# The place of a two-column sum in TensorE's queue: after the first transpose of a group, or in front of the product of its third tile

## The chip, the cores and the metric

One Trainium2 chip, one of its cores. The metric is the device time of the kernel in microseconds (us); less is better. Engines are called by their short names: PE (TensorE), DVE (VectorE), ACT (ScalarE), POOL (GpSimd) and SP (SyncE, which issues the loads). Line numbers (L1210) are those of the kernel before.

## The reference

The input `x` has 16 channels of 2048 x 2048 float32, in 8 groups of two channels. Two layers follow one another:

```python
# layer 0: group norm, causal mask, depthwise 6 x 11 convolution, mask, residual
xm = jnp.where(causal_mask, gn(x), 0)
y  = conv(xm, weight, padding=((5, 0), (5, 5)), feature_group_count=C)
x  = x + jnp.where(causal_mask, y, 0)
# layer 1: group norm again, plus a bias that depends on (row - column) only
m, s = mean(x_group), var(x_group)
x  = x + (x - m) / sqrt(s + 1e-5) + table[row - column]
```

Each of the two normalisations needs a mean and a variance over a whole group (two channels). The "second statistics" are those of layer 1: they can be had only when the last tile of the group has been through the convolution.

## The kernel before

A channel is cut into 4 bands of 512 rows, each band into overlapping tiles of 128 columns; only tiles that touch the lower triangle are convolved. That makes NT = 90 tiles for a group and 720 in all, numbered N = 90 g + n. The engines work as a pipeline in a common order written out by hand: `stage(s)` runs over n = 0 to 89, and in it a group s is being loaded and measured (its first statistics), group s-1 is being convolved, and group s-2 is finished (second normalisation, bias, store). So each stage has one seam, where the tiles of one group end and those of the next begin.

For each tile: ACT normalises it into `xn` (L647, four tiles ahead), POOL multiplies the mask into it where the tile lies on the diagonal (L1084), PE transposes it into `psT` (L1170, two tiles ahead), ACT copies the result as float16 into `XT` (`split_hi`, L659), DVE writes the rest of the float32 value beside it (`split_lo`, L801), POOL copies the halo columns (L1099, L1110), PE multiplies (the "product", 36 matmuls, L1184, into one of three `psY`), and DVE masks and adds the result to x (`evict`, L814 and L816). DVE also takes the first statistics from loaded buffers (L829) and does part of the finishing (L991, L1002). ACT squares and sums the finished blocks (`piece`, L679).

PE's queue takes tiles in triples. For a triple that begins at tile N it is: transpose N+2, product N, transpose N+3, product N+1, transpose N+4, product N+2. The product of tile N waits for `split_lo` of tile N and for the eviction of tile N-3; the transpose of tile N waits for its `xn` and for `split_lo` of tile N-3.

What ties the seam together, with "first" for the first tile of the new group:

- DVE, at n = 0: evict the old group's last tile, `split_lo` of tile first+2, sum of the tiles' sums (L924), one pair of L829. At n = 1 (STATS2): `stats2` part 0 (L935 to L944; waits for ACT's last squares, ends with the increment of `s2_chain` that PE waits for), then `split_lo` of tile first+3 (L801), then `stats2` part 1 (L949 on, waits for `s2_summed`), part 2 (the inverse root, with ACT's square root L753 in the middle, then L959, L960 and the shift of the kept bias, L964), then the eviction of tile first.
- ACT, at n = 1: the last squares (`piece`), `split_hi` of tile first+3, the norm of tile first+5, the square root, the shift of the bias (L699). At n = 2: `split_hi` of tile first+4.
- PE: `sum_results` (L1210) multiplies the two columns of `t2` by a matrix of ones, which sums them over the 128 partitions. In the trace it is two matmul records.
- SP: the loads go in order into a ring of 8 buffers of 512 KB (L566), beside the kept blocks (L572) and the bias (L602); a load waits for its buffer's last use.

There are 8 sums of this kind. Seven of them (groups 0 to 6) are issued in the first triple of the following group; the last stands alone at the end of PE's queue.

Of the kernel before, what the change touches and what calls it, by code (L numbers as in the profile page):

```python
# [25 lines left out]
def preact_conv_kernel(nc, x, wflip, w1, b1, w2, b2, w3, b3, out):  # L26
# [23 lines left out]
    NB3 = 3  # L50
# [257 lines left out]
    with ctx:  # L308
# [839 lines left out]
        def _(pe):  # L1148
# [16 lines left out]
            def transpose(N, m):  # L1165

                wait(pe, lo_ready, N - NB3 + 1)
                pe.wait_ge(xn_ready, N + 1)
                for i in range(NPC):
                    last = nc.tensor.transpose(psT[m][:, i, :], xn[:, m, i, :, :].rearrange("p k c -> p (k c)"), ident[:, :])  # L1170
                last.then_inc(transposed, 1)

            def convolve(N, m, c):
                pe.wait_ge(lo_ready, N + 1)
                pe.wait_ge(halo_in, N + 1)
                wait(pe, evicted, N - NB3 + 1)
                products = [(i, sh, xp, wp) for i in range(NPC) for sh in range(3)
                            for xp, wp in ((0, 0), (0, 1), (1, 0))]
                for j, (i, sh, xp, wp) in enumerate(products):
                    lo_c = max(0, PADC - XC * i)  # L1180
                    hi_c = min(WC, TOUT + PADC - XC * i)
                    rows = min(K, NE - K * sh)
                    o = XC * i - PADC
                    last = nc.tensor.matmul(psY[m][:, 0:rows, o + lo_c:o + hi_c],  # L1184
                                            XT[:, m, xp, i, 2 - sh:2 - sh + P],
                                            wsplit[:, c, wp, K * sh:K * sh + rows, lo_c:hi_c],
                                            start=(j == 0), stop=(j == len(products) - 1), skip_group_check=True)
                last.then_inc(convolved, 1)

            def triple(N, c, ahead=NB3, results_of=None):  # L1190

                for i in range(NB3):
                    if i < ahead:
                        transpose(N + i + 2, (i + 2) % NB3)
                    if i == 0 and results_of is not None:
                        sum_results(results_of)
                    convolve(N + i, i, c)

# [9 lines left out]
            def sum_results(g):  # L1208
                pe.wait_ge(s2_chain, 13 * g + 4)
                nc.tensor.matmul(total[:, 2:4], ones[:, :], t2[:, 0:2], start=True, stop=True).then_inc(s2_summed, 1)  # L1210

            def group(g, before, after):

                first = NT * g
                pe.wait_ge(w_built, chan(g, 0) + 1)
                triple(first, 0, results_of=g - 1 if before else None)
                with pe.Fori(1, NTC // NB3) as j:
                    triple(first + NB3 * j, 0)
                pe.wait_ge(w_built, chan(g, 1) + 1)
                triple(first + NTC, 1)  # L1220
                with pe.Fori(NTC // NB3 + 1, SUM1[0] if after else 2 * NTC // NB3 - 1) as j:
                    triple(first + NB3 * j, 1)
                if after:
                    triple(first + NB3 * SUM1[0], 1)
                    sum_means(g + 1)
                    triple(first + NB3 * SUM1[1], 1)
                    sum_variances(g + 1)
                    with pe.Fori(SUM1[1] + 1, 2 * NTC // NB3 - 1) as j:
                        triple(first + NB3 * j, 1)
# [37 lines left out]
```

## Time and profile before

| | |
|---|---|
| time, median of 3 runs | 2635.06 us (2629.83 to 2635.5) |
| the profiled execution: its own time | 2638.45 us |
| its span, first to last instruction | 2636.7 us |
| DVE busy | 2304.3 us, 87% |
| PE busy | 1979.8 us, 75% |
| ACT busy | 1660.3 us, 63% |
| POOL busy | 1260.7 us, 48% |
| moved by DMA | 894.88 MB, mean 339 GB/s |
| mean granted clock of PE | 0.912 of full speed |

How to read it: the shares are means over the span. A stage of the middle lasts 313 us or so, and which engine holds it changes inside the stage, so the table alone says nothing of a seam. Rows of the timeline give the start and the length of an instruction (or of several alike, with their count), and in brackets the idle time of its engine before it and what ended it.

### The profile page before, as it was taken

The numbers are of one execution on the slowest core, as the hardware profiler recorded it, in microseconds if no ns is written. First come the engines' busy times: TensorE is split into PE (matmuls) and PEld (weight loads), VectorE is DVE, ScalarE is ACT, GpSimd is POOL, SyncE is SP. The second block draws the span as 40 slices with busy tenths as digits, with TensorE's granted clock in tenths as the row PEclk, the third lists the DMA queues.
The fourth block names the chain that finished last, engine by engine and source line by source line (L and its number), as shares of the span: only waits on it lengthen the run. The fifth ranks groups of instructions, "written<-read, shape, count | busy, mean of one in ns | idle before, by whom it ended". The sixth has DMA issues, their size and how long they took to land. (4 is left out here: it accounts for less than half of the span.)

```text
span 2636.7 us, 76763 instructions
## 1 busy us (share of the span) xinstructions
PE 1979.8 (75%) x28880; PEld 1876.5 (71%) x28880; DVE 2304.3 (87%) x4175; ACT 1660.3 (63%) x3051; POOL 1260.7 (48%) x1988
## 2 busy tenths in 40 slices
PE   4289988888687876878778877888868778899800
PEld 0289887878687776877778776787768778899800
DVE  7799988899888997899888998889988899778846
ACT  2167766766576675766667666666656757687722
POOL 1123235535545454454555445554554546475543
PEclk9999998999899999999898999999889998999955
DMA  9775649999899998999989998999989997797999
GB/s 337 273 243 170 233 136 384 393 371 351 329 408 377 380 337 332 402 359 385 354 334 396 359 366 329 378 392 362 348 329 395 384 373 297 284 355 274 334 370 360
DMA packets 313546, 894.88 MB, mean 339 GB/s; under 512 B 42272, under 2 KB 42272, under 8 KB 311296
## 3 DMA queue, kind: packets, MB, share of 16 engines
q1 hardware_dynamic: 198528, 576.64, 59.3%
q10 hardware_dynamic: 114832, 316.22, 31.0%
q8 instruction: 60, 0.98, 0.1%
q14 instruction: 126, 1.03, 0.1%
HBM read 576.36 MB, written 316.53 MB: 339 GB/s over the span
## 5 line engine op out<-in xcount | busy, mean ns | idle before, releaser
L1184 PEld LDWEIGHTS psY<-wsplit,XT 128*128 128x128 f16 x25920 | 1607.2, 102 | 355.9 <-DVE XT L801 128.6
L1184 PE MATMUL psY<-wsplit,XT 128*128 128x168 f16 (+5 forms) x25920 | 1635.9, 223 | 290.7 <-DVE XT L801 240.2
L659 ACT CAST XT<-psT 128x512 f16<-128x512 f32 x720 | 414.8, 576 | 561.0 <-PE psT L1170 325.5
L1110 POOL COPY halo<-XT 128x16 f16<-128x16 f16 x720 | 318.9, 443 | 657.5 <-DVE XT L801 647.3
L801 DVE TENSOR_TENSOR XT<-psT,XT 128x512 f16<-128x512 f32 x720 | 493.8, 686 | 140.3 <-ACT XT L659 139.4
L1084 POOL TENSOR_TENSOR xn<-xn,mask 128x512 f32<-128x512 f32 x336 | 423.7, 1261 | 387.5 <-ACT xn L647 325.8
L829 DVE BATCH_NORM_STATS2 entries<-ring 128x6 f32<-128x512 f32 x872 | 551.4, 679 | 61.3 <-DMA ring<-in_x 61.0
L1170 PE MATMUL psT<-ident,xn 128*128 128x128 f32 x2880 | 480.3, 292 | 98.2 <-POOL xn L1084 77.6
L1119 POOL TENSOR_TENSOR ring<-ring,bias 128x1024 f32<-128x1024 f32 x181 | 408.4, 2258 | 253.7 <-ACT ring L708 253.6
L647 ACT ACTIVATE xn<-kept_c_band,normp 128x512 f32<-128x512 f32 (+2 forms) x496 | 398.4, 803 | 48.3 <-DMA kept_c_band<-in_x 26.9
L1170 PEld LDWEIGHTS psT<-ident,xn 128*128 128x128 f32 x2880 | 317.8, 146 | 107.4 <-POOL xn L1084 72.5
L816 DVE SCALAR_TENSOR_TENSOR kept_c_band<-psY,wback,kept_c_band 128x472 f32<-128x472 f32 (+3 forms) x496 | 342.5, 691 | 14.2 <-PE psY L1184 7.3
L679 ACT ACTIVATE junk<-kept_c_band,cur 128x512 f32<-128x512 f32 (+2 forms) x464 | 311.6, 672 | 49.5 <-DVE kept_c_band L816 26.2
L991 DVE SCALAR_TENSOR_TENSOR kept_c_band<-kept_c_band,outp,bias 128x1024 f32<-128x1024 f32 x224 | 329.2, 1478 | 11.6 <-ACT bias L699 11.6
L708 ACT ACTIVATE ring<-ring,outp 128x1024 f32<-128x1024 f32 x181 | 206.0, 1140 | 124.1 <-DMA ring<-in_x 48.0
L814 DVE TENSOR_TENSOR psY<-psY,mask 128x472 f32<-128x472 f32 (+2 forms) x336 | 202.8, 604 | 11.7 <-PE psY L1184 11.4
L1002 DVE SCALAR_TENSOR_TENSOR ring<-ring,outp,bias 128x1024 f32<-128x1024 f32 x101 | 173.9, 1724 | 33.2 <-DMA ring<-in_x 24.3
L1099 POOL COPY XT<-halo 128x16 f16<-128x16 f16 x720 | 159.9, 222 | 51.4 <-PE psY L1184 47.4
L647 ACT ACTIVATE xn<-band,normp 128x512 f32<-128x512 f32 (+1 forms) x224 | 174.3, 779 | 13.9 <-DVE normp L911 13.9
L816 DVE SCALAR_TENSOR_TENSOR band<-psY,wback,band 128x472 f32<-128x472 f32 (+2 forms) x224 | 150.4, 671 | 6.3 <-PE psY L1184 0.7
L679 ACT ACTIVATE junk<-band,cur 128x512 f32<-128x512 f32 x192 | 131.9, 687 | 36.3 <-DVE band L816 27.1
L679 ACT ACTIVATION_READ_ACCUMULATOR junk<-kept_c_band,cur 128x1 f32 x464 | 87.1, 188 | 0.0
(81 smaller groups left out, 486.2 us busy)
## 6 DMA issues: line engine op xcount, KB each, us to landing
ring<-in_x SPq DMA_DIRECT2D x628, 512.0 KB, 8.6
out<-ring ACTq DMA_DIRECT2D x282, 512.0 KB, 6.1
kept_c_band<-in_x SPq DMA_DIRECT2D x224, 512.0 KB, 8.1
out<-kept_c_band ACTq DMA_DIRECT2D x224, 512.0 KB, 7.0
band<-in_x SPq DMA_DIRECT2D x48, 1024.0 KB, 11.3
out<-band ACTq DMA_DIRECT2D x45, 1024.0 KB, 8.7
ring<-out SPq DMA_DIRECT2D x90, 512.0 KB, 9.5
bias<-bias_scratch SPq DMA_DIRECT2D x16, 1793.5 KB, 8.5
```

The costliest lines, as they stand in the source:

```text
L647: last = nc.scalar.activation(to[:, :, 0:whole, :], slot(c, b)[:, :, x0:x0 + XC * whole].rearrange("p k (i c) -> p k i c", c=XC), ACT.Iden ...
L659: nc.scalar.copy(XT[:, n % NB3, 0, :, 2:P + 2], psT[n % NB3][:, :, :]).then_inc(hi_ready, 1)
L679: nc.scalar.activation(junk[:, 0:nr * (c1 - c0)].rearrange("p (r c) -> p r c", r=nr), slot(c, b)[:, r:r + nr, BW * q + c0:BW * q + c1], AC ...
L801: nc.vector.tensor_tensor(XT[:, n % NB3, 1, :, 2:P + 2], psT[n % NB3][:, :, :], XT[:, n % NB3, 0, :, 2:P + 2], ALU.subtract).then_inc(lo_r ...
L816: nc.vector.scalar_tensor_tensor(out=xs, in0=y, scalar=col(wback, c), in1=xs, op0=ALU.mult, op1=ALU.add, accum_out=sums[:, n:n + 1]).then_ ...
L829: last = nc.vector.bn_stats(entries[:, e, :], row(q, r))
L991: nc.vector.scalar_tensor_tensor(out=v, in0=v, scalar=col(outp, 0), in1=bias_at(blk, nr // 2 * h, nr // 2), op0=ALU.mult, op1=ALU.add).the ...
L1084: nc.gpsimd.tensor_tensor(v, v, m, ALU.mult).then_inc(xn_ready, 1)
L1110: nc.gpsimd.tensor_copy(halo[:, t, :, :, :], XT[:, n % NB3, :, :, P:P + 2]).then_inc(halo_out, 1)
L1119: nc.gpsimd.tensor_tensor(v, v, bias_at(STREAM[u]), ALU.add).then_inc(u_added, 1)
L1170: last = nc.tensor.transpose(psT[m][:, i, :], xn[:, m, i, :, :].rearrange("p k c -> p (k c)"), ident[:, :])
L1184: last = nc.tensor.matmul(psY[m][:, 0:rows, o + lo_c:o + hi_c], XT[:, m, xp, i, 2 - sh:2 - sh + P], wsplit[:, c, wp, K * sh:K * sh + rows, ...
```

## The change

In `triple`, the sum is issued in front of the third product instead of the first. PE's queue in the first triple of groups 1 to 7 was: transpose first+2, sum, product first, transpose first+3, product first+1, transpose first+4, product first+2. It becomes: transpose first+2, product first, transpose first+3, product first+1, transpose first+4, sum, product first+2. Nothing else is changed: no other engine's queue, no wait, no buffer.

```diff
@@ -1192,7 +1192,7 @@
                 for i in range(NB3):
                     if i < ahead:
                         transpose(N + i + 2, (i + 2) % NB3)
-                    if i == 0 and results_of is not None:
+                    if i == NB3 - 1 and results_of is not None:
                         sum_results(results_of)
                     convolve(N + i, i, c)
```

## Rows read from the trace of the kernel before

**Rows 1.** Windows: the stage between the sums at 998 and 1311 us.

```profile
core 0: us, PE busy (x) PEld busy (x) DVE busy (x) ACT busy (x) POOL busy (x), PEclk, DMA share, GB/s
997.80:1311.30 313.50, 247.41 (x3606) 235.69 (x3606) 284.06 (x521) 205.45 (x379) 160.18 (x247) 0.92 0.96 364
```

**Rows 2.** Timeline of PE across the seam at 685 us.

```profile
674.23 0.64 PE L1170 MATMUL psT<-ident,xn 128*128 128x128 f32 x4
...
676.67 0.64 PE L1170 MATMUL psT<-ident,xn 128*128 128x128 f32 x4
685.03 0.58 PE L1210 MATMUL total<-t,ones 128*128 128x2 f32 x2 [7.72 <-DVE t L944]
685.48 3.76 PE L1184 MATMUL psY<-wsplit,XT 128*128 128x148 f16 x36
689.07 1.10 PE L1170 MATMUL psT<-ident,xn 128*128 128x128 f32 x4
...
696.82 2.13 PE L1184 MATMUL psY<-wsplit,XT 128*128 128x148 f16 x36 [1.69 <-DVE band L816]
```

**Rows 3.** Timeline of DVE, ACT and POOL across the same seam.

```profile
676.69 0.69 DVE L801 TENSOR_TENSOR XT<-psT,XT 128x512 f16<-128x512 f32 x1
...
679.79 0.69 DVE L801 TENSOR_TENSOR XT<-psT,XT 128x512 f16<-128x512 f32 x1
...
681.07 1.12 POOL L1084 TENSOR_TENSOR xn<-xn,mask 128x512 f32<-128x512 f32 x1 [2.95 <-ACT xn L650]
...
683.08 0.52 ACT L679 ACTIVATE junk<-kept_c_band,cur 128x310 f32<-128x310 f32 x1
...
684.83 0.15 DVE L944 SCALAR_TENSOR_TENSOR t<-t 128x1 f32<-128x1 f32 x1
...
690.82 0.69 DVE L801 TENSOR_TENSOR XT<-psT,XT 128x512 f16<-128x512 f32 x1 [5.85 <-ACT XT L659]
691.43 0.15 DVE L949 TENSOR_SCALAR t<-total 128x1 f32<-128x1 f32 x1
...
693.72 0.16 DVE L960 SCALAR_TENSOR_TENSOR outp<-t 128x1 f32<-128x1 f32 x1
```

**Rows 4.** Timelines of DVE at the six other seams, the same instruction.

```profile
379.07 0.69 DVE L801 TENSOR_TENSOR XT<-psT,XT 128x512 f16<-128x512 f32 x1 [5.85 <-ACT XT L659]
...
1003.59 0.69 DVE L801 TENSOR_TENSOR XT<-psT,XT 128x512 f16<-128x512 f32 x1 [5.85 <-ACT XT L659]
...
1316.42 0.69 DVE L801 TENSOR_TENSOR XT<-psT,XT 128x512 f16<-128x512 f32 x1 [5.16 <-ACT XT L659]
...
1630.10 0.69 DVE L801 TENSOR_TENSOR XT<-psT,XT 128x512 f16<-128x512 f32 x1 [5.42 <-ACT XT L659]
...
1944.49 0.69 DVE L801 TENSOR_TENSOR XT<-psT,XT 128x512 f16<-128x512 f32 x1 [5.13 <-ACT XT L659]
...
2253.41 0.69 DVE L801 TENSOR_TENSOR XT<-psT,XT 128x512 f16<-128x512 f32 x1 [5.86 <-ACT XT L659]
```

**Rows 5.** Windows after the seams at 998 and 2248 us, columns as in rows 1.

```profile
1007.80:1012.80 5.00, 3.32 (x51) 2.85 (x49) 4.93 (x13) 3.88 (x6) 0.02 (x1) 1.00 0.15 35
...
1002.80:1032.80 30.00, 23.11 (x349) 21.43 (x348) 28.27 (x57) 18.10 (x29) 16.67 (x19) 0.98 0.73 243
...
1037.80:1057.80 20.00, 14.11 (x215) 13.73 (x212) 13.04 (x24) 11.71 (x23) 7.59 (x14) 0.86 1.03 416
...
2247.60:2262.60 15.00, 13.62 (x175) 13.31 (x176) 8.36 (x24) 6.49 (x9) 1.79 (x5) 0.80 0.10 39
```

**Rows 6.** Waits over the span (us, times, longest), then timelines of DVE and PE.

```profile
DVE entries L829 <- DMA ring<-in_x: 61.0, 41, 6.1
...
1052.74 1.29 DVE L829 BATCH_NORM_STATS2 entries<-ring 128x6 f32<-128x512 f32 x2 [6.08 <-DMA ring<-in_x]
...
1055.72 3.54 PE L1184 MATMUL psY<-wsplit,XT 128*128 128x148 f16 x36 [3.87 <-DVE XT L801]
```

**Rows 7.** L602 alone, the bias load issued at 677.80 us.

```profile
DMA to landing us min/median/max: 10.0/10.0/10.0
```

## The prediction

> **What bounds the kernel now.** I read the page first, for the busy shares, then windows of whole stages. In a middle stage DVE works 284.06 of 313.5 us and the DMA engines are busy 0.96 of the time, while PE works 247.41 [rows 1]. So two things share the bound, DVE and the transfers. Windows of 5 to 30 us show that they take turns. In the 30 us behind the seam at 998 us DVE is busy 28.27 us and the DMA share is 0.73; from 1037.8 us the share is 1.03, which is as full as this trace gets over 20 us, and DVE falls to 13.04 of 20 us, waiting among other things 6.08 us for a load of the ring [rows 5, 6]. Neither explains the seam itself, so the timelines across a seam come next.
>
> At 685 us PE has stood still for 7.72 us when it reaches the sum [rows 2]. Its last work was the transpose of tile first+2 (676.67 us). It then waits for the chain of DVE that ends with L944 (684.83 us), although the product of tile first could have run: its `split_lo` had ended at 677.38 (676.69 + 0.69) [rows 3]. After the sum come that product, 3.76 us long, and the transpose of first+3, 1.10 us [rows 2]. Only then can ACT and DVE split tile first+3, and that split stands on DVE in front of `stats2` part 1. So DVE, which had nothing left to do at 684.98, idles 5.85 us, until 690.82 [rows 3]. The sum had long been ready. The reader is to see a loop of orders: PE's next product waits for DVE's chain, and DVE's next step waits for what stands behind that product. The other seams show the same idle time in front of the same instruction: 5.85, 5.85, 5.16, 5.42, 5.13 and 5.86 us [rows 4]. With 5.85 at 685 us that is 39.1 us of DVE idle at seven seams.
>
> **The change, step by step**, at the seam of 685 us. It adds and removes no instruction. The sum moves past two products and two transposes of PE's queue; it issues no transfer, and no other queue changes.
>
> 1. Product first starts at about 677.4 instead of 685.48. A tile (transpose and product overlapped) takes 2.44 us at full clock (676.67 less 674.23) [rows 2], so the transpose of first+3 starts at about 679.4 and ends at 680.0. Its `xn` is masked before that of first+4, which POOL has at 682.19 (681.07 + 1.12) [rows 3].
> 2. Product first+1 needs `split_lo` of first+1, done at 680.48 [rows 3]. It runs 680.5 to 682.6, and the transpose of first+4, whose `xn` is there, ends at 683.2.
> 3. The sum still waits for L944, so it starts at 685.03 as before, and takes 0.58 us [rows 2]: ready at 685.6. The wait on PE shrinks from 7.7 to 1.8 us. Behind it are product first+2 and the transpose of first+5; nobody needs them before DVE has gone through its chain.
> 4. ACT ends its last square at about 683.8 (683.08 + 0.52, and 0.19 for the read of the sum, estimated from the spacing of its squares) and copies first+3 by 684.4. DVE splits it right behind L944, 684.9 to 685.6. Part 1, at 691.43 before [rows 3], starts at 685.7. DVE has gained 5.7 us, its idle time less about 0.1.
> 5. Parts 1 and 2 and the eviction of tile first move up by the same 5.7 us. Queued behind part 1 on DVE are all of these; ACT's square root and bias shift wait for them, and so does product first+3, whose releaser is that eviction [rows 2]. Part 2 needs the bias in its place: that load lands 10.0 us after its issue at 677.80, at 687.8 [rows 7], and part 2 wants it after L960, then 693.88 less 5.73 = 688.15 [rows 3]. It is just there; this becomes the next thing to be late, with 0.3 us to spare.
>
> The edit to PE's own order I cost at nothing. What hides it is that PE waits for DVE behind the seam. Product first+3 would start at 691.1 (696.82 less 5.7) while PE is done with first+5 at about 688.1: an idle stretch of 3.0 us where it was 1.69 [rows 2]. A stretch of 3.87 us was followed by a product of 3.54 us, that is at 1.2 GHz for most of its length, against 2.13 us at 2.4 GHz [rows 2, 6]. If 3.0 us does the same, the tile takes 3.5 + 0.5 us; DVE needs about 4.3 us for a tile there, so the cover holds. Without cover it costs 1.4 us at each seam, 10 us in all.
>
> On this the Trainium skill (TensorE: Matmul & The Clock Gate, "HAM oscillation — how this bites in real kernels") warns that repeated idle gaps put the array back to half clock and that each pass pays for it again. By that rule the sum would lose those 10 us if PE set the pace behind a seam; the rows have DVE setting it there, and I go by the rows.
>
> For the first and the last of the seven the bound on the sum's delay is small: there L944 ends sooner after the last product, and PE would reach the sum 0 to 0.5 us after it. Gross over seven seams: 39.1, less 7 x 0.1, less 2 x 0.4 = 37.6 us.
>
> **What the transfers give back.** DVE's work is earlier, but the bytes are the same. Behind the last seam the DMA share is 0.10 over 15 us, and the first is alike in kind (few loads in flight) [rows 5]; there I keep all, 10.7 of the 37.6. Behind the five in the middle the share falls to 0.15 only for 5 us, once the loads in flight have landed; the next ones wait for buffers that DVE frees [rows 5]. Over the 30 us the idle room against 1.03 is (1.03 - 0.73) x 30 = 9.0 us. The pulled-forward work needs 5.4 us (26.9 over five) of it before the full stretch begins. The room suffices on paper, but a good part lies where DVE, not DMA, is full. Bounds: nothing lost (26.9 us kept in the middle) and everything lost (0). I take three quarters kept, near the upper end because the room is larger than the need: 20.2. Together 31 us. Against the profiled execution's 2638.45 that gives 2607.5; the median of the runs shown is 3.4 lower, so the forecast is 2635.06 - 31 = 2604.
>
> **Rivals.**
> - *Transfers take back the middle.* The 6.08 us wait for a load 50 us behind the seam [rows 6] grows by what was gained. For it: a share of 1.03 for 20 us in front of and across that wait, and 0.96 over the stage [rows 1, 5]. Against: the 9.0 us of room. Only the outer seams and a few us of the rest stay: about 14 us, 2621.
> - *The clock.* With PE started at a seam at 1.2 GHz, two products and transposes take 2 x (3.76 + 1.10) less overlaps = 9.4 us from 677.4, so the sum ends at 687.4 instead of 685.6. That loses 1.7 us at each of seven seams: 31 - 12 = 19 us kept, 2616. Against: PE no longer stands still there, products before it run at full clock.
> - *It does nothing measurable.* The stage's length would be set by transfers alone. Against: a share of 0.96 where 1.03 is reached leaves 313.5 x 0.07 = 21 us a stage. 2635.
> - *Slower.* One mechanism: loads and stores that now start into a still full queue land later, and L829, which waits 61.0 us in 41 places [rows 6], waits longer. It decides once the wait at such a place is more than 5.4 us longer in the middle stages and eats the outer seams too, that is from 37.6/5 = 7.5 us on, 13.6 where 6.08 stood. At 10 us: 5 x 10 - 38 = 12 slower, 2647. Nothing in the rows asks for so much.
>
> **Chances.** The forecast's case 0.68 (it contains the case of nothing given back, 2597.5), transfers take back the middle 0.13, the clock 0.10, nothing 0.05, slower 0.04. A difference of 0.2% (5.3 us) is about what a measurement of this kernel can tell from none. Faster by more than that: 0.91, within it 0.05, slower 0.04. The range reaches from the full gross gain, 2597.5, and a little for a bound missed, to the case where the middle is taken back: 2596 to 2622.
>
> **What would show it.** Right: PE's record of L1210 preceded by under 2.5 us idle; L801 in front of L949 with no idle (0 to 0.5 us) at seven seams; L944 to L949 under 1 us apart; the distance between two sums shorter by some 4 us in the middle (313.5 to 309). Step 1 wrong: product first does not run in front of the sum, or takes over 3 us. Step 5 wrong: a new idle time in front of L964 for the bias. The transfers' part wrong: the wait at L829 some 50 us behind a seam the same (nothing lost) or over 10 us (the middle lost). What would make the whole wrong is a wait in the new order that I did not follow, on POOL's halo copies above all, since they stand between the products.

## The result, and the profile after

The new kernel takes 2593.95 us (median of 4 runs, 2590.45 to 2599.09) against 2635.28 us before: a ratio of 0.9847, 95% interval 0.9832 to 0.9862, or 40.3 us less (36.4 to 44.3). Two more sets of five runs gave 37.4 us less (32.4 to 42.7) and 41.6 us less (37.7 to 45.6). The forecast was 2604, 31 us less, with 2596 as its fastest; the direction and the place were right, and the size was short by 9 us, of which 6.7 are the part that transfers were to take back. The profiled execution of the new kernel took 2592.56 us, with a span of 2590.8; that is 45.9 us under the profiled one of before, more than the medians are apart, since that of before was slower than any of the four timed.

PE's timeline across the same seam, now at 680 us, answers to [rows 2]:

```profile
674.55 0.64 PE L1170 MATMUL psT<-ident,xn 128*128 128x128 f32 x4
675.68 2.13 PE L1184 MATMUL psY<-wsplit,XT 128*128 128x148 f16 x36 [0.48 <-DVE XT L801]
...
680.17 0.38 PE L1210 MATMUL total<-t,ones 128*128 128x2 f32 x2 [1.88 <-DVE t L944]
680.41 2.12 PE L1184 MATMUL psY<-wsplit,XT 128*128 128x148 f16 x36
...
686.05 3.42 PE L1184 MATMUL psY<-wsplit,XT 128*128 128x148 f16 x36 [3.03 <-DVE band L816]
```

The products of tiles first and first+1 run in front of the sum at full clock (the one of 675.68 is first+1), PE waits 1.88 us for DVE's chain where it waited 7.72, and the sum comes right behind L944 as before. DVE's timeline answers to [rows 3]:

```profile
679.97 0.15 DVE L944 SCALAR_TENSOR_TENSOR t<-t 128x1 f32<-128x1 f32 x1
680.04 0.68 DVE L801 TENSOR_TENSOR XT<-psT,XT 128x512 f16<-128x512 f32 x1
680.64 0.14 DVE L949 TENSOR_SCALAR t<-total 128x1 f32<-128x1 f32 x1
...
682.94 0.16 DVE L960 SCALAR_TENSOR_TENSOR outp<-t 128x1 f32<-128x1 f32 x1
683.21 1.29 DVE L964 TENSOR_SCALAR bias<-bias,outp 128x2051 f32<-128x2051 f32 x1
```

L801 carries no idle time any more, and L949 starts 0.67 us behind L944's start where it started 6.60 us behind. The same holds at all seven seams, of which the first and the last are:

```profile
372.53 0.68 DVE L801 TENSOR_TENSOR XT<-psT,XT 128x512 f16<-128x512 f32 x1
...
2209.47 0.68 DVE L801 TENSOR_TENSOR XT<-psT,XT 128x512 f16<-128x512 f32 x1
```

Windows behind the seam and over the stage, to be read against [rows 1, 5]:

```profile
core 0: us, PE busy (x) PEld busy (x) DVE busy (x) ACT busy (x) POOL busy (x), PEclk, DMA share, GB/s
991.00:1021.00 30.00, 21.89 (x316) 20.49 (x316) 29.24 (x54) 18.37 (x31) 17.92 (x21) 0.94 0.98 347
986.90:1292.80 305.90, 241.14 (x3607) 228.72 (x3607) 283.01 (x522) 204.98 (x379) 158.46 (x247) 0.96 0.98 375
```

The first window begins 4.1 us behind the start of the sum, that of [rows 5] 5.0 us; with 5.0 us in both the share is the same 0.98. It was 0.73: the engines' idle room of 9.0 us has shrunk to (1.03 - 0.98) x 30 = 1.5 us. Over such windows behind all five middle seams the share was 0.73 to 0.82 before and is 0.93 to 0.99 now, in the mean 0.19 more, or 5.7 us. The stage is 7.6 us shorter (313.5 to 305.9). The six distances between the seven sums are shorter by 4.2 to 8.5 us, 6.2 in the mean, in this pair of profiles, where some 4 were forecast.

What the load queue of SP waits for behind the same seam says how the transfers moved. From 1000 to 1017 us before, and from 985 to 1001 us in the new kernel, it waits for one thing, the statistics of DVE that free the buffers of the ring:

```profile
SPq L445 <- DVE entries L829: 13.9, 2, 10.0
```

```profile
SPq L445 <- DVE entries L829: 9.5, 2, 5.7
```

So the loads there are released by DVE, and they go out earlier when DVE is earlier: the longest wait is 4.3 us shorter here, and 3.4 to 6.3 us shorter at the four other middle seams.

The waits of DVE for loads, over the whole span, in the new kernel's first profile and then in that of its second set of runs (named new_again below):

```profile
DVE entries L829 <- DMA ring<-in_x: 69.7, 38, 6.6
```

```profile
DVE entries L829 <- DMA ring<-in_x: 62.2, 36, 6.0
```

Against 61.0 us before [rows 6] that is 8.7 and 1.2 us more. Executions of one program differ here by as much as the term that I had forecast, so this row alone decides nothing. The waits that the forecast named do: those of L829 for a load some 50 us behind each middle seam. Read from the profiles' timelines, in the order of the seams:

| | us behind L944 | the five waits, us | together |
|---|---|---|---|
| before | 53 to 56 | 1.22, 6.08, 5.12, 5.10, 4.63 | 22.2 |
| new kernel | 46 to 50 | 5.82, 1.39, 6.57, 5.18, 5.41 | 24.4 |
| new_again | 46 to 49 | 2.29, 5.73, 4.64, 5.71, 1.88 | 20.3 |
| new_third | 46 to 50 | 2.04, 3.57, 6.30, 6.40, 2.23 | 20.5 |

They end some 6 us earlier behind L944, about what DVE has gained, and they are as long as before. Had transfers taken back all of the middle, they would be 27 us longer together, and 6.7 us with the quarter that was forecast.

### The profile page after: what moved, and what is told of

It is laid out like the page before. It is cut to its first block, busy times and chain, and to the rows that moved or that the text cites. A ratio compares the mean times of both kernels' runs of the same rounds, so it can differ in the third digit from the quotient of the medians.

```text
span 2590.8 us, 76763 instructions
## 1 busy us (share of the span) xinstructions
PE 1956.0 (75%) x28880; PEld 1851.3 (71%) x28880; DVE 2295.2 (89%) x4175; ACT 1658.5 (64%) x3051; POOL 1249.8 (48%) x1988
## 2 busy tenths in 40 slices
DMA packets 313546, 894.88 MB, mean 345 GB/s; under 512 B 42272, under 2 KB 42272, under 8 KB 311296
## 3 DMA queue, kind: packets, MB, share of 16 engines
q14 instruction: 126, 1.03, 0.1%
## 4 chain that ended last, share of the span: by engine, by line
DVE 44%; DMA 25%; PE 11%; issue 10%; ACT 5%; POOL 3%; ACTq 1%; SPq 1%; POOLq 0%; DVEq 0%
DVE entries L829 13%; DMA ring<-in_x 11%; PE psY L1184 8%; DVE XT L801 7%; DVE kept_c_band L991 7%; DMA out<-ring 5%; DVE kept_c_band L816 5%; DVE psY L814 4%; DVE ring L1002 3%; DMA out<-kept_c_band 3%; DMA out<-band 3%; PE psT L1170 2%; DVE band L816 2%; ACT junk L679 2%; ACT xn L647 2%
## 5 line engine op out<-in xcount | busy, mean ns | idle before, releaser
L1184 PEld LDWEIGHTS psY<-wsplit,XT 128*128 128x128 f16 x25920 | 1583.5, 101 | 361.5 <-DVE XT L801 123.2
L1184 PE MATMUL psY<-wsplit,XT 128*128 128x168 f16 (+5 forms) x25920 | 1612.8, 221 | 296.2 <-DVE XT L801 237.2
L1110 POOL COPY halo<-XT 128x16 f16<-128x16 f16 x720 | 310.6, 431 | 660.7 <-DVE XT L801 649.9
L1084 POOL TENSOR_TENSOR xn<-xn,mask 128x512 f32<-128x512 f32 x336 | 429.5, 1278 | 392.6 <-ACT xn L647 332.2
L829 DVE BATCH_NORM_STATS2 entries<-ring 128x6 f32<-128x512 f32 x872 | 551.4, 679 | 70.2 <-DMA ring<-in_x 69.7
L801 DVE TENSOR_TENSOR XT<-psT,XT 128x512 f16<-128x512 f32 x720 | 493.3, 685 | 97.6 <-ACT XT L659 96.9
L991 DVE SCALAR_TENSOR_TENSOR kept_c_band<-kept_c_band,outp,bias 128x1024 f32<-128x1024 f32 x224 | 324.3, 1456 | 12.4 <-ACT bias L699 12.4
L1002 DVE SCALAR_TENSOR_TENSOR ring<-ring,outp,bias 128x1024 f32<-128x1024 f32 x101 | 170.2, 1686 | 34.3 <-DMA ring<-in_x 27.3
L1099 POOL COPY XT<-halo 128x16 f16<-128x16 f16 x720 | 151.4, 210 | 7.7 <-PE psY L1184 4.3
```

What stands on the lines that cost most here:

```text
L801: nc.vector.tensor_tensor(XT[:, n % NB3, 1, :, 2:P + 2], psT[n % NB3][:, :, :], XT[:, n % NB3, 0, :, 2:P + 2], ALU.subtract).then_inc(lo_r ...
L829: last = nc.vector.bn_stats(entries[:, e, :], row(q, r))
L991: nc.vector.scalar_tensor_tensor(out=v, in0=v, scalar=col(outp, 0), in1=bias_at(blk, nr // 2 * h, nr // 2), op0=ALU.mult, op1=ALU.add).the ...
L1084: nc.gpsimd.tensor_tensor(v, v, m, ALU.mult).then_inc(xn_ready, 1)
L1110: nc.gpsimd.tensor_copy(halo[:, t, :, :, :], XT[:, n % NB3, :, :, P:P + 2]).then_inc(halo_out, 1)
```

## The experiments

All ratios are to the kernel before, run on the same chip, with five to twelve runs of each version; differences are the ratio times the median of before in that set.

**The new kernel again (new_again, new_third).**

> The changed kernel once more, for a tighter interval. Theory A (each seam gives back DVE's whole idle time, transfers take nothing): 37.6 to 38.5 us less than the kernel before. Theory B (transfers take back part of the five middle seams, as forecast): 31 us less. Theory C (the seams set off a further gain elsewhere in the stages, beyond the idle time removed): over 41 us less.

> The new kernel on the same chip as evict_early and dose_small, for comparison: 37 to 40 us less than before.

Measured: 0.9858 (0.9838 to 0.9877), 37.4 us less, and 0.9842 (0.9827 to 0.9857), 41.6 us less. The first fits the gross sum of 37.6, and 31 lies below its interval; the second has 37.6 just outside its lower edge. Nothing taken back fits both within 0.1 us; a further gain of 2 to 4 us is neither shown nor excluded.

**Some seams only (outer_seams, middle_seams).** `place` is a new argument of `triple`, the i at which the sum is issued.

```diff
-                triple(first, 0, results_of=g - 1 if before else None)
+                triple(first, 0, results_of=g - 1 if before else None,
+                       place=NB3 - 1 if g in (1, G - 1) else 0)   # outer_seams
+                       place=0 if g in (1, G - 1) else NB3 - 1)   # middle_seams
```

> The sum is moved at the first and the last of the seven seams only. Theories A and B: 10.7 to 11.5 us less than before, the idle time of DVE at these two. Theory C: more than that, 13 us or over, if the extra comes from these seams.

> The sum is moved at the five middle seams only. Theory A: 26.9 us less than before (27.4 of idle less 0.1 each). Theory B: 20 us less, or down to 3 if transfers take back nearly all. Theory C: 30 us or more.

Measured: outer 0.9959 (0.9944 to 0.9974), 10.8 us less (6.8 to 14.7), where 10.7 were forecast. Middle: 0.9881 (0.9861 to 0.9901), 31.3 us less (26.1 to 36.6), where 26.9 are the idle time and 20.2 were forecast as kept. So the error sits in the middle seams: the forecast's 20.2 is outside the interval, the whole idle time inside. So are the 30 us and more of Theory C; the outer seams show none of its further gain. The two parts add up to 42.1, no more than the whole allows.

**DVE's wait removed another way (split_behind_stats).**

```diff
-                    lo_first = do_c and n == STATS2
+                    lo_first = False
```

> PE's queue is that of the kernel before; on DVE the second split of tile first+3 goes behind the whole of stats2 and the eviction of tile first, so that part 1 does not wait for PE's product. If DVE's idle time alone is the cost (theory A in its narrow form), nearly all of the gain comes here too: 30 us or more less. If PE's late start at the seam (7.7 us idle, then half clock) counts as well, PE is the next to be late, since product first+3 could start at 695 instead of 691 us at the seam of 685: 7 x (5.7 - 4) = 12 us less, and DVE idle in front of the evictions of tiles first+1 and first+2.

Measured: 0.9998 (0.9985 to 1.001), the same: 0.5 us less, between 2.6 more and 3.9 less. The profile shows why neither expectation held. DVE's timeline behind the sum (part 1 there starts at once, at 685.09), then ACT's:

```profile
685.86 0.15 DVE L954 TENSOR_SCALAR t<-t 128x1 f32<-128x1 f32 x1
691.13 0.16 DVE L865 RECIPROCAL t<-t 128x1 f32<-128x1 f32 x1 [5.12 <-ACT t L753]
```

```profile
689.64 0.59 ACT L659 CAST XT<-psT 128x512 f16<-128x512 f32 x1 [6.48 <-PE psT L1170]
...
690.84 0.19 ACT L753 ACTIVATE t<-t 128x1 f32<-128x1 f32 x1
```

The chain goes through ACT's square root, which stands behind the copy of tile first+3, and this waits 6.48 us for the transpose behind PE's first product. The idle time of 5.85 us has only moved inside the chain, as 5.12 us and 0.68 us more in front of part 1, for the sum itself. I had overlooked the second link of the same kind, so this run doesn't answer its question.

**Both links removed, PE as before (root_first).** The same edit, and on ACT:

```diff
+                    if do_c and n == STATS2:
+                        act.wait_ge(s2_root, gc * 2 + 1)
+                        nc.scalar.activation(t2[:, 6:7], t2[:, 5:6], ACT.Sqrt).then_inc(s2_root, 1)
                     if n + 2 < NT:
                         if do_b:
                             split_hi(gb, n + 2)
...
                         if n == STATS2:
-                            act.wait_ge(s2_root, gc * 2 + 1)
-                            nc.scalar.activation(t2[:, 6:7], t2[:, 5:6], ACT.Sqrt).then_inc(s2_root, 1)
                             act.wait_ge(gn2_ready, gc + 1)
```

> As split_behind_stats (PE's queue of the kernel before, DVE's split of tile first+3 behind stats2), and on ACT the square root now stands in front of the copy of tile first+3, so that no part of DVE's chain stands behind PE's first product. Theory 'the idle time of DVE was the cost, PE's late start was not': most of the gain of the new order, 30 to 38 us less than before. Theory 'PE's late start at the seam counts as well': PE becomes the next to be late, and 15 us or less is gained.

Measured: 0.9886 (0.9868 to 0.9904), 30.0 us less (25.3 to 34.7). PE in this kernel still stands idle 7.49 us in front of the sum and still runs the next product at half clock:

```profile
680.25 0.58 PE L1211 MATMUL total<-t,ones 128*128 128x2 f32 x2 [7.49 <-DVE t L945]
680.70 3.76 PE L1185 MATMUL psY<-wsplit,XT 128*128 128x148 f16 x36
```

So most of the gain is there with PE as late as before. Two rows of DVE say where the rest may be:

```profile
680.87 0.16 DVE L950 TENSOR_SCALAR t<-total 128x1 f32<-128x1 f32 x1 [0.68 <-PE total L1211]
...
694.15 2.35 DVE L992 SCALAR_TENSOR_TENSOR kept_c_band<-kept_c_band,outp,bias 128x1024 f32<-128x1024 f32 x1
```

With the split moved away nothing covers the sum's own time, 0.68 us at each of seven seams, 4.8 us; and one operation on a kept block takes 2.35 us where its neighbour takes 1.27, while POOL adds a bias in the ring (693.04 to 695.42). The same operation takes 1.90 to 2.47 us at four of the seven seams, 4.0 us too much in all. The first of the two is part of the design. That the second explains the remainder was not tested, and over the whole span it is doubtful: the operations of this kind together take 33 us more than 1.27 us each here, and 33 us in sum_second on the same chip, which gains 38.4 us.

**One product earlier or later (sum_second, sum_last).** `place=1`, and the sum behind the loop of `triple`.

> The sum in front of the second product, one product earlier than in the new kernel. The transpose of tile first+3 is already out, so DVE has no idle time in front of part 1, but PE stands still for 4 to 5 us in front of the sum and its next products run at half clock for some us. If only DVE's idle time counts: 37 us less than before, as the new kernel. If PE's lateness counts: 25 to 32 us less.

> The sum behind the third product, one product later than in the new kernel. At the seam of 685 us that product would run 683.2 to 685.3, while the sum is waited for until 685.0 anyway: DVE's part 1 is 0.3 us later at the middle seams and 2.1 us later at the outer two, so 7 x 0 to 2.1 of the new kernel's gain is lost: 32 to 37 us less than before. PE's idle stretch in front of product first+3 would grow from 3.0 to 5 us, which costs nothing if DVE sets the pace there and 10 us if PE does.

Measured: 0.9854 (0.9837 to 0.9871), 38.4 us less, and 0.986 (0.9841 to 0.9879), 36.8 us less: as the new kernel. What PE does at the two seams is very unlike. First sum_second, then sum_last:

```profile
679.78 0.58 PE L1212 MATMUL total<-t,ones 128*128 128x2 f32 x2 [4.98 <-DVE t L944]
680.23 3.76 PE L1184 MATMUL psY<-wsplit,XT 128*128 128x148 f16 x36
```

```profile
684.63 0.38 PE L1212 MATMUL total<-t,ones 128*128 128x2 f32 x2
...
690.51 3.78 PE L1184 MATMUL psY<-wsplit,XT 128*128 128x148 f16 x36 [4.94 <-DVE band L816]
```

In both, PE idles nearly 5 us here and takes 1.6 us longer for a product at half clock, once in front of the sum and once behind it, and neither shows in the time. What the three places have in common is that the transpose of first+3 is in front of the sum. One cost of sum_last is too small for these runs: at the two outer seams DVE waits 1.44 and 1.45 us for the sum, 2.9 us together.

**DVE work put back at the seam (dose_dve, dose_small).**

The buffer `spare`, which takes the results, is new and not shown here.

```diff
                     if do_c and n == STATS2:
+                        for k in range(9):   # 4 in dose_small
+                            nc.vector.bn_stats(spare[:, k, :], mask[:, 0:BW])
                         stats2(gc, 1)
```

> The new kernel with nine added statistics operations on DVE (on a constant, results unused) in front of part 1 of each stats2, 5 to 6 us of DVE work at each of eight seams; PE's order is the new one. Theory A (DVE's time at the seam passes one to one into the total, transfers take nothing): 37.5 less, 8 x 5.7 more: 4 to 10 us above the kernel before. Theory B (transfers hide a part in the middle): 5 to 15 us below the kernel before.

> As dose_dve with four added operations, 2.4 us at each of eight seams, 19 us in all. One to one: 18 to 20 us less than before. If transfers hid the first few us in the middle stages: 25 to 35 us less.

In the trace of dose_dve the nine take 5.43 us with their overlap at the ends, and delay part 1 by 5.34 us (690.44 to 695.78):

```profile
690.44 5.43 DVE L1024 BATCH_NORM_STATS2 spare<-mask 128x6 f32<-128x512 bf16 x9
695.78 0.14 DVE L950 TENSOR_SCALAR t<-total 128x1 f32<-128x1 f32 x1
```

At seven seams that is 37.4 us, and at the eighth sum, where DVE waited 0.68 us for the sum anyway, 4.6: 42.0 us. Measured: 1.0016 (1.0005 to 1.0026), 4.2 us above the kernel before, hence 41.6 us above new_again (or 44.5 above the first set of the new kernel), with some 6 us of uncertainty; the new kernel was not run on the chip of this set. dose_small: 0.9919 (0.9904 to 0.9933), 21.3 us less, against 41.6 less for new_third on the same chip: 20.3 us, with some 5.5 of uncertainty, for a dose that delays part 1 by 18.3 us (2.38 at each of seven, 1.63 at the eighth). The slope is 1 at both sizes, within some 15 and 30%. Transfers hide no part of DVE's work at the seam that these runs can measure.

**Fewer bytes (light_old, light_new).** The stores of finished kept blocks write their first 128 columns only, in the kernel before and in the new one; the rest of those results is left out.

```diff
+                few = slice(0, BW // 4)
-                act.dma_start(part(ov[chan(g, c), b], blk, half * h, half), part(kept[(c, b)], blk, half * h, half)
-                              ).then_inc(kept_stored[(blk, h)], 16)
+                act.dma_start(part(ov[chan(g, c), b], blk, half * h, half)[:, :, few],
+                              part(kept[(c, b)], blk, half * h, half)[:, :, few]).then_inc(kept_stored[(blk, h)], 16)
```

> The kernel before with the stores of the finished kept blocks cut to their first 128 columns (an eighth or a quarter of each; the rest of those results isn't written): some 90 to 100 of 895 MB less. Theory 'DVE's time at the seam passes on whole because transfers do not set the length of a stage': this kernel is only as much faster as DVE waited for transfers and lost by them, 10 to 60 us, and the idle time at the seams stays 5 to 6 us each. Theory 'transfers set the length': 100 of 895 MB at the full rate of some 413 GB/s, over 200 us less.

> The same cut in the new kernel. If transfers took nothing of the gain in the full kernels, the distance between this and light_old is the same 37 to 40 us as between the full ones. If they took a part there and less here, the distance is larger here, over 42 us.

Measured: 0.9798 (0.9774 to 0.9822), 53.2 us less, and 0.9621 (0.9608 to 0.9634), 99.9 us less. 894.88 MB have become 794.22. At the 416 GB/s of a full stretch [rows 5] those 100.7 MB are 242 us of transfer. The profiles agree: the packets of the store queue take 31.0% of 2636.7 us before and 22.4% of 2573.6 us in light_old, 241 us less. Those of the load queue take 42 us more. Only 53 us come out: bytes cost something, but they don't set the length. DVE's waits for ring loads, in light_old and then in light_new:

```profile
DVE entries L830 <- DMA ring<-in_x: 31.0, 14, 4.6
```

```profile
DVE entries L830 <- DMA ring<-in_x: 26.4, 14, 4.7
```

Half the waits of [rows 6] are gone, and the idle time of DVE at the seams of light_old is still 5.40 to 5.85 us each. The distance of the two is 46.6 us by the ratios, with some 7 us of uncertainty, and 36.6 us by the spans of their profiles (2573.6 and 2537.0). The median is above the 42 that I had set as the mark for "transfers took a part in the full kernels", the interval and the spans reach below it. For a part of a few us this pair is inconclusive.

**PE released earlier behind the seam (evict_early).**

```diff
                     if do_c and n == STATS2:
+                        if do_b:
+                            evict(gb, n - 1)
                         stats2(gc, 1)
...
                     if n >= 1:
-                        if do_b:
+                        if do_b and not (do_c and n == STATS2):
                             evict(gb, n - 1)
```

> The new kernel with DVE's eviction of tile first in front of part 1 of stats2 instead of behind part 2. DVE's work is the same, but PE's product first+3 is released some 4 us earlier, so PE has no idle stretch of 3.0 us at the seam and no product at half clock there. If DVE sets the pace behind the seam (as forecast), the time is that of the new kernel: 37 to 40 us less than before. If PE's idle stretch and its slow product cost something (the clock rival), 45 to 50 us less.

Measured: 0.9853 (0.9829 to 0.9877), 38.7 us less (32.4 to 45.1), as new_third (41.6). The product of first+3 starts 2.7 us behind the start of the sum instead of 5.9; at the seam of 678 us it runs at full clock:

```profile
678.49 2.12 PE L1186 MATMUL psY<-wsplit,XT 128*128 128x148 f16 x36
...
680.93 2.13 PE L1186 MATMUL psY<-wsplit,XT 128*128 128x148 f16 x36
```

At this seam the product of 3.42 us of the new kernel is gone, and the time over all seams is the same. But the idle time has moved rather than gone: PE now waits some 2.3 us for ACT's `xn` and 0.8 to 1.3 us for L801 a little later, and at four of the seven seams the product behind that takes 3.4 to 3.8 us. So the run shows that PE's release of first+3 was not the pace; it does not take away the slow product that nearly every seam has in every version. No version here that writes the whole result is faster than the new kernel beyond the intervals.

## Why the prediction was right and where it failed

**The loop of orders** was read rightly, and the steps at the seam came out to a tenth: PE's wait in front of the sum 1.88 us (forecast 1.8), L949 right behind the split, PE's idle stretch behind it 3.03 us (3.0) with a product of 3.42 us (3.5). root_first shows it from the other side: with PE as late as before, taking DVE's chain out from behind PE's first product gives 30.0 us. PE's rows came out so at this seam; at others the product at half clock is the one right behind the sum, or there is none (in new_third 3.02 us idle at the last seam, then 2.13 us). What I had not named is that two links of DVE stood behind that product, the split on DVE and the square root behind ACT's copy; moving the sum cuts both at once, and split_behind_stats, which cuts one, gains nothing measurable.

**The gross sum**, 37.6 us, lies in the intervals of two of the three sets of the new kernel (32.4 to 42.7 and 36.4 to 44.3) and 0.1 us outside that of the third (37.7 to 45.6). **The outer seams** gave 10.8 us for 10.7.

**The step that failed** is "I take three quarters kept" of the middle seams: 6.7 us that transfers were to take back. They took nothing that can be measured: the middle seams gave 31.3 us (26.1 to 36.6) where 20.2 were forecast, the waits for loads 50 us behind them are 20.3 to 24.4 us together where they were 22.2, and doses of DVE work at the seam pass into the time one to one. The quarter itself was a choice; no row gave it. The working had the answer in it. The idle room of the DMA engines was computed at 9.0 us against a need of 5.4, and in the new kernel 5.7 us of such room are filled in the mean of the five seams. I discounted it because DVE, not DMA, is full there, but that is what makes the loads able to move: the load queue waits for DVE there, so the loads come earlier when DVE does. The waits some 50 us behind the seam moved with their stage instead of growing. The one of 6.08 us even reads 1.39 us in the first profile of the new kernel:

```profile
1032.42 1.28 DVE L829 BATCH_NORM_STATS2 entries<-ring 128x6 f32<-128x512 f32 x2 [1.39 <-DMA ring<-in_x]
```

In new_again it is 5.73 us and in new_third 3.57 at the same place, while other seams are longer than before, so 1.39 is one execution's, and no gain. The fast end of the range was then 1.5 us beyond the gross sum, with nothing in it for the scatter of a median (2587.74 to 2599.14 in one set of five), and the result fell 2 us outside. The remaining 2.7 us between 37.6 and 40.3 lie inside the interval and are not explained.

**The rivals.** That transfers take back the middle is refuted by middle_seams, the waits and the doses. The clock rival's condition did not come: the product in front of the sum ran in 2.13 us, not 3.76. Nor does the slow product behind the sum reach the time. In the three profiles of the new kernel DVE waits for PE at none of the seven seams in the 27 us behind L944 (waits of over 0.1 us counted), and only 0.3 us for ACT's square root; PE's idle time and its slow product lie under DVE's work. sum_second and sum_last, with nearly 5 us idle, agree. The warning of the Trainium skill (TensorE: Matmul & The Clock Gate, "HAM oscillation — how this bites in real kernels") describes what most of these rows show, an idle stretch (3.03 us) and then a product at 1.2 GHz for most of its length (3.42 us for 2.13), and in this case the trace agrees with it on the clock at most seams. But PE isn't the pace here, so the penalty doesn't reach the total. **The bias** had 0.3 us to spare by my reckoning and arrives just in time or a little late: L964 waits for it once in the new kernel, 0.25 us, and once in new_again, 0.17 us.

**What stays open.** Whether the new order gains 2 to 4 us beyond the idle time removed. The three sets give 37.4, 40.3 and 41.6, the light pair 46.6 +- 7; none of them excludes 37.6 by much. One place where executions differ by as much is DVE's own busy time: 2304.3 us before, and 2295.2, 2302.1 and 2297.5 us in the three profiles of the new kernel; in the first of these most of the difference lies in two operations on finished blocks (L991 324.3 us where it was 329.2, L1002 170.2 where it was 173.9; on L991 see the last section). split_behind_stats, which is as slow as the kernel before, has 2300.9, so these profiles do not show that the new order changes it.

## What to carry to other kernels

When an engine idles in front of an instruction, follow the order of each queue on the way round, not just the semaphore that ended the wait: here PE's small sum held up a product whose transpose held up the very engine that produced the sum's successor. Before moving one of the links, list all that hang behind the same instruction, since cutting one of two gained nothing here. And where transfers and an engine take turns as the bound, look at the stretch behind the stall and not at the mean DMA share of the stage. Here the idle room was larger than the gain and the load queue waited for that same engine, and the stall passed on whole. One kernel shows this; where the room is smaller than the gain it was not tested.

## What was not expected of the hardware

An operation of DVE on a kept block (L991, 128x1024 float32) takes 1.27 to 1.29 us in most places, and 2.35 us at one place of root_first. It is not an accident of that run. POOL and DVE there, and at one place of the kernel before:

```profile
693.04 2.38 POOL L1120 TENSOR_TENSOR ring<-ring,bias 128x1024 f32<-128x1024 f32 x1 [1.72 <-ACT ring L708]
694.15 2.35 DVE L992 SCALAR_TENSOR_TENSOR kept_c_band<-kept_c_band,outp,bias 128x1024 f32<-128x1024 f32 x1
```

```profile
909.82 2.37 POOL L1119 TENSOR_TENSOR ring<-ring,bias 128x1024 f32<-128x1024 f32 x1 [1.88 <-ACT ring L708]
911.12 2.15 DVE L991 SCALAR_TENSOR_TENSOR kept_c_band<-kept_c_band,outp,bias 128x1024 f32<-128x1024 f32 x1
```

Both times DVE's operation ends 1.08 us behind the end of POOL's. The same holds, to 0.02 us, for 38 of the 39 such operations of between 1.35 and 4 us in the kernel before, 27 of 28 in the new one and 38 of 39 in root_first; the three others begin within 0.06 us of the start of an operation of POOL. Since 1.08 us is nearly the whole length of DVE's operation alone, these rows look as if it gets almost nothing done while POOL's still runs. In the kernel before this costs 32 us over the span, in the profiles of the new kernel 27 to 32. Which operations meet depends on the order of the other engines, and a forecast by durations from the trace of before can't see that.
